# A vision tower with a state-space layer and a mixture of experts: the pairwise addition of states moves from DVE to POOL

## The reference

```python
h = tower(x)                                # patches of 16 -> 197 tokens x 128, two transformer blocks
h = layernorm(h + mamba(h, f) + flip(mamba(flip(h), b)))
h = layernorm(h + experts(h))               # 64 experts, 8 per token, at most 256 tokens each

def mamba(x, ...):                          # 128 channels, 16 states, 197 tokens in sequence
    ...
    dA  = exp(dt[..., None] * A)
    dBx = dt[..., None] * Bm[:, :, None, :] * xs[..., None]
    _, h = associative_scan(comb, (dA, dBx), axis=1)
    y = einsum('blds,bls->bld', h, Cm) + D * xs     # the sum over the 16 states
```

## Time and profile before

| what | value |
|---|---|
| median of 3 runs | 9048.21 us (9047.15 to 9054.67) |
| the profiled execution | 9069.71 us, of which the span of the profile is 9067.5 |
| busy share of the span | PE 78%, DVE 78%, ACT 68%, POOL 10% |
| a step with routing, a step without | 144.79 us, 126.55 us |
| granted clock of PE, whole span | 0.912 |

### The profile page before, as it was taken

One profiled execution on the slowest core, in us unless ns is written; L12 is line 12 of the kernel. 1 busy time (PEld: TensorE's weight loads), 2 busy tenths in 40 slices (PEclk: granted clock), 3 DMA queues, 4 the chain that ended last, 5 costly groups with the idle time before them and its releaser, 6 DMA issues. The chain is left out here.

```text
span 9067.5 us, 118721 instructions
## 1 busy us (share of the span) xinstructions
PE 7087.1 (78%) x33290; PEld 3932.2 (43%) x33290; DVE 7049.0 (78%) x9161; ACT 6179.6 (68%) x13424; POOL 884.1 (10%) x657
## 2 busy tenths in 40 slices
PE   6777777788888888888888888888888888887442
PEld 3444444444444444444444444444444444443221
DVE  2788888888888888888888888888888888887423
ACT  5666666677777777777777777777777777775114
POOL 0124242300000000000000000000000000000373
PEclk9898898999999999999999999999999999998555
DMA  3232222233333333233333333333333333323335
GB/s 124 102 110 96 104 101 99 104 111 117 113 116 113 115 117 113 105 120 117 111 116 110 111 117 115 120 111 111 117 113 112 113 119 117 113 100 117 88 61 145
DMA packets 283717, 1005.40 MB, mean 111 GB/s; under 512 B 45448, under 2 KB 135404, under 8 KB 275052
## 3 DMA queue, kind: packets, MB, share of 16 engines
q1 hardware_dynamic: 248556, 981.23, 30.2%
q0 software_dynamic: 34816, 21.19, 1.6%
HBM read 938.66 MB, written 63.58 MB: 111 GB/s over the span
## 5 line engine op out<-in xcount | busy, mean ns | idle before, releaser
L1056 PE MATMUL psS<-KM,Q 128*99 128x394 f32 x4096 | 1733.1, 540 | 344.6 <-ACT PTs L607 254.1
L862 DVE TENSOR_TENSOR_SCAN hs<-dA,hs 128x1576 f32<-128x1576 f32 x512 | 1762.3, 3442 | 63.0
L601 ACT ACTIVATE P<-psS,least_s 99x197 f32<-99x197 f32 x4096 | 1414.8, 431 | 477.4 <-DVE least_s L787 469.7
L1063 PE MATMUL psS<-cst,P 99*99 99x99 f32 x8192 | 1048.6, 269 | 347.0 <-ACT P L601 302.5
L1063 PEld LDWEIGHTS psS<-cst,P 99*99 99x99 f32 x8192 | 914.4, 176 | 896.8 <-ACT P L601 652.5
L787 DVE TENSOR_REDUCE least_s<-psS 99x2 f32<-99x394 f32 x2048 | 1087.5, 562 | 273.6 <-PE psS L1056 241.2
L678 ACT ACTIVATE dA<-dt_,aneg 128x394 f32<-128x394 f32 x2048 | 1185.0, 621 | 29.0 <-DVE hs L862 18.9
L607 ACT ACTIVATE PTs<-psS 99x396 f32<-99x396 f32 x2048 | 984.9, 517 | 225.5 <-PE psS L1063 220.7
L1056 PEld LDWEIGHTS psS<-KM,Q 128*99 128x99 f32 x4096 | 629.9, 175 | 1085.8 <-ACT PTs L607 575.5
L848 DVE TENSOR_TENSOR hs<-hs,u 128x1576 f32<-128x1576 f32 x512 | 917.4, 1792 | 41.6 <-DMA hs<-bc_scratch 40.7
L1148 PE MATMUL psY<-hs,cst 128*128 128x394 f32 x2048 | 825.4, 533 | 121.7 <-DVE hs L871 121.4
(11 more groups left out here) (195 smaller groups left out, 9646.3 us busy)
## 6 DMA issues: line engine op xcount, KB each, us to landing
hs<-bc_scratch SPq DMA_DIRECT2D x512, 788.0 KB
cr<-bc_scratch SPq DMA_DIRECT2D x512, 788.0 KB
pat<-patches SPq DMA_DIRECT2D x64, 1176.0 KB, 6.0
rows_scratch<-zeros SPq DMA_DIRECT2D x1, 19104.0 KB, 62.2
sum_scratch<-HW SPq DMA_DIRECT2D x64, 148.5 KB
hs<-sum_scratch SPq DMA_DIRECT2D x15, 512.0 KB
out<-hs SPq DMA_DIRECT2D x15, 512.0 KB, 2.9
bc_scratch<-dtbc SPq DMA_DIRECT2D x128, 49.2 KB
```

The costliest lines, as they stand in the source:

```text
L601: last = nc.scalar.activation(P[:, r, b, m, 0:T], psS[0:CT, 2 * r + b, m * T:(m + 1) * T], ACT.Exp, bias=least_s[:, r, b, m:m + 1], scale= ...
L862: nc.vector.tensor_tensor_scan(h, a, h, 0.0, ALU.mult, ALU.add).then_inc(scan_ready, 1)
L1056: mm(psS[0:CT, 2 * r + b, 0:2 * T].rearrange("p (e t) -> p e t", e=2), Q[:, r, b, q * CT:(q + 1) * CT], KM[:, r, h % 2 * 2:h % 2 * 2 + 2, ...
L1063: last = nc.tensor.transpose(psS[0:CT, 2 * r + b, at:at + CT], P[:, r, b, m, k * CT:(k + 1) * CT], c("ident")[0:CT, 0:CT])
```

## The change

The function `half` moves from DVE's block to POOL's. It waits for the same product (`mul_done`), adds the same elements and signals the same semaphore. It keeps its place in the order of the units, which POOL reads from DVE's list. Nothing else is changed.

```diff
             def route_unit(i):
                 while_open(pool, i, pool_waited, pool_read, route)
                 pool.sem_inc(slots_free, 1)
...
+            def half(i, g):
+                pool.wait_ge(mul_done, i * MULS + MUL_OUT[g])
+                pool.sem_inc(pool_waited, 1)
+                nc.gpsimd.tensor_tensor(hs[:, g % HBUF, 0:2, :], hs[:, g % HBUF, 0:2, :], hs[:, g % HBUF, 2:4, :], ALU.add).then_inc(half_summed, 1)
...
-            loop(pool, "dve", {}, {"keep": keep, "route": route_unit})
+            loop(pool, "dve", {}, {"keep": keep, "half": half, "route": route_unit})
...
-            def half(i, g):
-                dve.wait_ge(mul_done, i * MULS + MUL_OUT[g])
-                nc.vector.tensor_tensor(hs[:, g % HBUF, 0:2, :], hs[:, g % HBUF, 0:2, :], hs[:, g % HBUF, 2:4, :], ALU.add).then_inc(half_summed, 1)
...
-                  "half": half, "ys": ys, "merge": merge, "route": route_unit})
+                  "ys": ys, "merge": merge, "route": route_unit})
```

## The result

| kernel | median us | range | runs |
|---|---|---|---|
| before | 9048.44 | 9047.15 to 9054.67 | 4 |
| after | 9499.55 | 9496.79 to 9502.01 | 4 |

The ratio is 1.0497, with a 95% interval of 1.0479 to 1.0515: 451 us longer. The profiled execution of after took 9496.79 us, its span is 9494.9.

A forecast was written before the change was run, and what follows sets the result against it. No engine was full; PE, DVE and ACT were close together, handing small attention tiles to each other. Ten stops of 43 us (+430) and 0 for the other steps, on the median 9048, gave 9478 us; range 9290 to 9660.

The forecast's parts named there:

- Place and chain of the stop: In ten steps with routing, half 0 on POOL waits for 32 transfers; PE stops at sum 0, then ACT and DVE.
- Its length: PE's stop per step with routing: half 0 done at 757.3, PE resumes 43.2 us late; ten stops cost +430 us.
- the upper bound of 772.7: All transfers as slow as before, ended at 767.6, with upper addition price and landing 772.7: a stop of 58.6 us.
- The clock and what is given back: At each stop's end: PE restarting at low clock costs +1.9 us; DVE and ACT being ahead gives 1.9 back.
- The steps without routing: The 54 steps and the rest of those with routing: between +1 and -1 us a step, taken as 0.
- The 7.7 us removed from DVE: Eight additions of 0.96 us a step leave DVE; about 1.0 gained without mutual holding, the rest beside ACT and PE work.
- Rival A: DVE was the bound, offload pays in steps without routing: 9233 at half of 7.7 us, 9318 at 2.5; chance 0.14.
- Rival B: POOL and DVE exclude each other; each of 8 halves holds DVE 1.8 us: 3.4 us a step, 9693; chance 0.12.
- C: Stops in steps with routing longer, 60 us, 9650, chance 0.07; or shorter, 35 us, 9398, chance 0.03.
- D: Faster: all of DVE's saving on the path, needing over 6.7 us a step; 8986 at the full 492; chance 0.04.

The follow-up runs named there:

- Experiment 8: The changed kernel's edit for half 0 alone: half 0 on POOL, the other seven halves on DVE; 9463.86 us, ratio 1.0460.
- Experiment 1: The changed kernel with halves 0 to 3 back on DVE, only 4 to 7 on POOL, each group with its own semaphore; 9064.62 us, ratio 1.0013.
- 3: The changed kernel, all halves on POOL, with the 32 transfers issued in four parts of 8, each behind one of halves 0 to 3; 9113.91 us, ratio 1.0078.
- Experiment 4: The changed kernel with only 8 of the 32 transfers in each step with routing, the other 24 left out; 9180.77 us, ratio 1.0146.
- experiment 11: The kernel before, unchanged, profiled a second time; 9057.35 us, a step without routing 126.32 us.
- experiment 6: The kernel before with no halves at all: DVE only signals, states 2 and 3 of each quarter left out of the sum; 9002.29 us, ratio 0.9949.
- experiment 5: The kernel before, DVE keeping its halves, with two unused 128x394 additions of constants on POOL at each same place; 9397.01 us, ratio 1.0382.
- experiment 2: The changed kernel with half 0 back on DVE, halves 1 to 7 on POOL; 9551.64 us, ratio 1.0550.
- Experiment 10: The changed kernel's edit for halves 1 and 2 only: these on POOL, the others on DVE; 9440.77 us, ratio 1.0440.
- experiment 7: The kernel before, DVE keeping its halves, with four 128x400 memsets on POOL at each same place, writing SBUF and reading none; 9047.51 us, ratio 1.0001.

## Why the prediction was right

**Place and chain of the stop: shown.** `Half 0` behind the last landing, PE ahead of sum 0, DVE and ACT behind PE. Experiment 8 has it with half 0 alone, 1 is free of it without halves 0 to 3, and 3 all but removes it by the order of POOL's queue.

**Its length: 43.2 us forecast, 42.0 measured.** Term by term: 25 undisturbed transfers where I had 24; landing 1.59 us for the assumed 2; the addition 1.82 for the assumed 1.8, a price that no row of before could show. Experiment 4 confirms the price of a transfer: 31.1 us less waiting for 24 fewer. Two slips of the working are small: 24 x 1.29 is 31.0 and not 31.1, and the upper bound of 772.7 holds 3.0 us for the landing and the semaphores, of which the text names 2.3.

**The clock and what is given back: forecast +1.9 and -1.9.** The granted clock is 0.50 in the stop and still from 1034 to 1036, 1.00 from 1038 to 1040. That PE waits 42.0 us and the step grows by 42.6 leaves 0.6 for both together. The two were not measured apart.

**The steps without routing: 0 forecast, between +1 and -1.** Measured -0.03 against the execution of experiment 11. The 7.7 us removed from DVE were too many: an instruction behind a `half` starts 0.87 us after it (4009.74 to 4010.61 in the step of the earlier trace rows), and without halves DVE is busy for 6.5 us less. That it came out to a few hundredths is luck: the forecast took 0 as a middle between a gain (if the engines don't exclude each other) and a loss (if they do), and had nothing in it of the granted clock, which fell from 0.96 to 0.95 in these steps while at the same clock they were 1.4 us shorter. Exclusion is real, in both directions, as the text had it for half 2 and for `SG` (0.9 forecast, 1.03 measured). That also takes the mean of an addition to 2375 ns, outside the 1.1 to 2.1 us forecast for it; undisturbed it is 1.85. In after it costs DVE, by the means from 3000 to 8000 (scans 3481, `small` 1158, `SG` 1084 ns), 8 x 0.039 + 2 x 0.800 + 2 x 0.521 = 3.0 us a step; by the windows it is busy for 102.0 us in place of 105.4, a net relief of 3.4. None of it shows in the mean step, and of the 6.5 us of experiment 6 only 0.2 does, while experiment 5 goes the other way, 6.1 us more for DVE and 5.6 for the step. One reading is that before, DVE stood just at the edge of being the bound, so that relief is worth nothing and a load counts in full. The table by clock speaks against it as the whole account: between steps of the same clock the relief is worth 1.4 us (after) and about 2 (experiment 6), and the load costs 2.2 to 3.8. How much is DVE's place and how much the clock was not separated.

**Rival A (DVE was the bound)** asked for 2.5 to 3.8 us a step from 7.7. With no halves at all the mean step gains 0.2, and about 2 at the same clock: DVE is in part on the path, but the time doesn't get it. **Rival B (DVE pays each time)** had the mechanism right and its price wrong: DVE pays 3.0 us where B took 8 x 1.8, since most additions fall beside reductions of PSUM or idle time (argued from the rows), and where a scan has just begun POOL pays first. **C**: the longest of the ten stops is 43.1 us, their mean 42.0. **D** needed 6.7 us a step, and no run comes near it.

**What the sum had left out.** 430 were forecast and the medians differ by 451. Between the two spans of the table the difference is 440: 426 for the ten steps, as forecast, and 14 in the last two steps and the rest, which the prediction gave no term. In the last step the attention is no longer beside the state-space layer, and DVE goes from an output straight into the next scan and input. POOL and DVE there:

```profile
8839.06 4.96 POOL L511 TENSOR_TENSOR hs<-hs 128x788 f32<-128x788 f32 x1 [6.40 <-DVE hs L872]
```

```profile
8838.94 3.44 DVE L867 TENSOR_TENSOR_SCAN hs<-dA,hs 128x1576 f32<-128x1576 f32 x1
8842.30 3.39 DVE L853 TENSOR_TENSOR hs<-hs,u 128x1576 f32<-128x1576 f32 x1
```

The addition begins with the scan and comes to its turn after it, as DVE's own did, but then it takes twice as long, PE waits for it, and DVE's next input is held for 1.6 us. Three inputs, one output, one scan and one scalar operation of that step are held so, by 1.3 to 1.6 us each, 9.1 us together. That this makes up the 14 us is argued from these rows, not shown by a run. The 11 us that then lack to 451 are the distance of the two single executions from their medians: 9057.35 is 8.9 over, 9496.79 is 2.8 under.

**Still open** is experiment 2's step without routing, 128.38 us. Experiment 1 rules out that halves 4 to 7 on POOL do it by themselves. Experiment 10 is no such clear answer: at a clock of 0.95 its steps take 128.2 us, as those of 2 do (127.9) and those of before (127.7), where after's take 126.3. Its mean is lower because 38 of its 50 steps are granted more. So a part of the 2.1 us goes with the clock (0.94 in the mean in 2, 0.95 in after), and the rest is that 2 lacks what makes after's steps shorter at the same clock; what that is wasn't tried.

## What to carry to other kernels

An operation that moves to another engine enters that engine's queue behind everything there, so read what the new queue does in its rarest and longest branch. A batch of 32 transfer issues ahead of one addition, in 10 of 64 steps, outweighed 492 us of relief. Before making room on an engine, run the kernel with the work simply left out: here that run says 46 us, a tenth of what the change cost. And where a relief doesn't reach the time, compare the granted clock of the same step before and after, since here the steps of a relieved DVE came with a lower one.

## What was unexpected of the hardware

POOL's addition of 128x788 takes 1.85 us undisturbed, but 4.96 to 5.06 when a DVE scan has started just before it; DVE's scan takes up to 4.97 us for 3.44 and a 0.36 us scalar operation 1.96 when POOL is first. A POOL `memset` (128x400, 0.43 us at the median) over a scan lengthens neither, but where it meets the `SG` scalar operation, which came first each time between 3000 and 8000 us, it takes over 0.5 us, 0.90 in the row of experiment 7. An indirect transfer's issue on POOL, 0.98 us alone, is stretched too, to 5.33 us in experiment 2, beside three DVE operations with both inputs in SBUF. Two short additions on POOL held DVE's scans, `SG` and `small` off by 3.0 us a step in experiment 5, as one long one did in after; the 1.8 more of experiment 5 fall on the halves, which in after aren't on DVE. And steps of one kernel with the same work differ by 7 us, from 123.2 to 130.4, with the granted clock of the step.
